# GpSimd's two gathers of a step, moved from the step's head to behind its first and second subtraction

## What is computed

```python
e = jnp.stack([tbl_0[ids[:, 0]], ..., tbl_31[ids[:, 31]]], axis=1)      # 1024 x 32 x 64
for i in range(2):                                                       # x0 = h = e
    z = jnp.einsum('bhd,bmd->bhmd', h, x0).reshape(batch, H * M, dim)
    out = jax.nn.relu(jnp.einsum('bcd,oc->bod', z, Ws[i]) + bs[i][None, :, None])
    # first layer: out[:, :64] is the next h, out[:, 64:] is a result; second: all of out
z = jnp.sum(jnp.concatenate(finals, axis=1), axis=-1)
h = jnp.concatenate([z, dense_ctx], axis=1)
h = relu(h @ W_top1 + b_top1); h = relu(h @ W_top2 + b_top2); y = h @ W_top3
```

## Time and profile before

| | |
|---|---|
| median of three runs | 1965.58 us (1965.43 to 1966.08) |
| the profiled execution | 1965.55 us, span 1963.7 us |
| PE busy | 1929.8 us (98%) |
| DVE busy | 1914.1 us (97%) |
| POOL busy | 1826.8 us (93%) |
| ACT busy | 1729.9 us (88%) |
| POOL L299, subtractions | 384, 1581.7 us |
| POOL L265, gathers from `idx` | 240, 228.3 us |

### The profile page before, as it was taken

How to read it: one execution, slowest core, us unless ns; L and a number is a source line. 1 busy time by engine, 2 the same in 40 slices (tenths; PEclk the granted TensorE clock), 3 DMA queues, 4 the chain that set the end, 5 groups by cost and what they waited for, 6 DMA issues and landing times.

```text
span 1963.7 us, 28730 instructions
## 1 busy us (share of the span) xinstructions
PE 1929.8 (98%) x7240; PEld 1361.8 (69%) x7240; DVE 1914.1 (97%) x1246; ACT 1729.9 (88%) x1959; POOL 1826.8 (93%) x646
## 2 busy tenths in 40 slices
PE   3999999999999999999999999999999999999999
PEld 2667777777776776776776777677677677677776
DVE  5999999999999999999999999999999999999995
ACT  4889998998998998998899899899899899889986
POOL 4999999999999999999999999999999999999883
PEclk8999999999999999999999999999999999999999
DMA  8987777777777777787787787787778777777730
GB/s 215 239 212 188 198 187 186 196 191 184 194 194 181 196 193 180 194 194 186 192 196 187 185 197 192 181 196 194 181 193 197 183 191 194 188 187 196 187 93 1
DMA packets 277281, 364.27 MB, mean 185 GB/s; under 512 B 116353, under 2 KB 116737, under 8 KB 277138
## 3 DMA queue, kind: packets, MB, share of 16 engines
q1 hardware_dynamic: 265730, 352.74, 72.7%
q0 software_dynamic: 8192, 8.40, 1.9%
q10 hardware_dynamic: 3344, 2.96, 0.6%
HBM read 347.02 MB, written 16.78 MB: 185 GB/s over the span
## 4 chain that ended last, share of the span: by engine, by line
PE 96%; DMA 1%; ACT 1%; POOL 1%; DVE 1%; issue 1%; ACTq 0%; DVEq 0%
PE out L814 22%; PE out L839 21%; PE out L833 21%; PE out L832 21%; PE out L822 7%; PE out L816 2%; POOL zl L299 1%; PE hrep L880 0%; DMA xrep<-fields_dram 0%; DMA left_x<-fields_dram 0%; ACT hrep L486 0%; ACT zh L473 0%; PE xr L880 0%; PE lz L880 0%; DVE zl L774 0%
## 5 line engine op out<-in xcount | busy, mean ns | idle before, releaser
L299 POOL TENSOR_TENSOR zl<-prod,zh 128x2048 fp32r<-128x2048 f32 (+2 forms) x384 | 1581.7, 4150 | 45.2 <-ACT zh L473 43.3
L832 PE MATMUL out<-zh,w1h 128*128 128x512 f32 x1888 | 736.6, 390 | 0.8 <-ACT relu L479 0.8
L833 PE MATMUL out<-zh,w1l 128*128 128x512 f32 x1888 | 736.7, 390 | 0.0
L473 ACT ACTIVATE zh<-prod 128x2048 fp32r<-128x2048 f32 (+2 forms) x384 | 664.9, 1732 | 17.3 <-DVE prod L719 9.4
L486 ACT ACTIVATE hrep<-out,b_sb 32x512 f32<-32x512 f32 (+1 forms) x768 | 496.2, 646 | 139.2 <-PE out L816 129.4
L839 PE MATMUL out<-zl,w1h 128*128 128x512 f32 x1888 | 565.9, 418 | 0.6 <-POOL zl L299 0.6
L814 PE MATMUL out<-prod,w_sb 128*128 128x512 f32 x1024 | 464.8, 597 | 27.2 <-DVE prod L650 22.3
L839 PEld LDWEIGHTS out<-zl,w1h 128*128 128x128 f32 x1888 | 354.4, 188 | 128.6 <-issue 61.5
L832 PEld LDWEIGHTS out<-zh,w1h 128*128 128x128 f32 x1888 | 354.7, 188 | 103.3 <-issue 30.4
L833 PEld LDWEIGHTS out<-zh,w1l 128*128 128x128 f32 x1888 | 354.4, 188 | 76.4
L814 PEld LDWEIGHTS out<-prod,w_sb 128*128 128x128 f32 x1024 | 195.2, 191 | 224.4 <-issue 214.6
(11 more groups left out here) (69 smaller groups left out, 721.3 us busy)
## 6 DMA issues: line engine op xcount, KB each, us to landing
rot_low<-fields_dram SPq DMA_DIRECT2D x512, 256.0 KB, 6.2
rot_high<-fields_dram SPq DMA_DIRECT2D x512, 256.0 KB, 4.2
xrep<-fields_dram SPq DMA_DIRECT2D x252, 128.0 KB
left_y<-fields_dram SPq DMA_DIRECT2D x256, 64.0 KB, 2.2
fields_dram<-emb SPq DMA_DIRECT2D x504, 32.0 KB, 4.5
left_x<-fields_dram SPq DMA_DIRECT2D x252, 64.0 KB, 2.3
emb<-in_tables,idx POOLq DMA_INDIRECT x244, 3.6
w_sb<-in_w SPq DMA_DIRECT2D x1, 1024.0 KB, 5.8
```

Source lines behind the costliest of these rows:

```text
L299: pool.tensor_tensor(zl[u][:, 0:size, :], product[:, 0:size, :], zh[u][:, 0:size, :].bitcast(F32), ALU.subtract).then_inc(zl_made[u], 1)
L473: act.activation(zh[u][:, 0:size, :], product[:, 0:size, :], ACT.Copy).then_inc(zh_made[u], 1)
L832: nc.tensor.matmul(out1[:, :], w1h[:, k, :], zh[u][:, t, :], start=start and t == 0, stop=False)
L833: nc.tensor.matmul(out1[:, :], w1l[:, k, :], zh[u][:, t, :], start=False, stop=False)
```

## The change

In `step` of GpSimd, `gathers` is called twice with one gather each instead of once with two. Of the step's two gathers the first now stands behind the subtraction of part 0 and the second behind that of part 1. The waits of an even step (`scratch_written`, `idx_loaded`) and the increment of `gather_started` go with its first gather. Step 0 had its first subtraction ahead of the gathers already. Nothing changes on another engine, and no instruction is added or removed.

```diff
-            def gathers(i, c):
+            def gathers(i, c, k):
                 n, b = i * 2 + c // 2 + AHEAD, (c // 2 + AHEAD) % 2
                 if known(i) and n == AHEAD:
-                    if c % 2 == 0:
+                    if c % 2 == 0 and k == 0:
                         pool.wait_ge(scratch_written[b], AHEAD // 2 * WRITTEN)
                     rows = known_rows(n)
                 else:
-                    if c % 2 == 0:
+                    if c % 2 == 0 and k == 0:
                         pool.wait_ge(scratch_written[b], written(b, i + (c // 2 + AHEAD) // 2))
...
-                for g in range(c % 2 * 2, c % 2 * 2 + 2):
-                    gather(b, rows, g)
+                gather(b, rows, c % 2 * 2 + k)
...
-                first = known(m) and m == 0
-                if first:
-                    low_part(0, 0, in_parts(0, 0), prod[1])
-                if is_up_to(i, c, LAST - 2 * AHEAD):
-                    gathers(i, c)
-                if not first:
-                    low_part(m, 0, in_parts(0, c), prod[1])
+                gathering = is_up_to(i, c, LAST - 2 * AHEAD)
+                low_part(m, 0, in_parts(0, c), prod[1])
+                if gathering:
+                    gathers(i, c, 0)
                 low_part(m, 1, in_parts(1, c), prod[2])
+                if gathering:
+                    gathers(i, c, 1)
                 low_part(m, 2, in_parts(2, c), prod[3])
```

## The result

The changed kernel took 1984.88 us (median of six runs, 1984.05 to 1985.55), the kernel before 1965.67 us (1965.28 to 1966.08). The ratio of the two is 1.0098 with a 95% interval of 1.0088 to 1.0108: 19.2 us slower. The forecast was 1981.7 us.

The account below looks back on a forecast made before the run. TensorE, without a gap in a 59.31 us turn, was taken to set the pace, with GpSimd nearly as full. 30 turns x 0.54 = 16.2 us added to 1965.55 gave 1981.7 us, range 1965.3 to 1992.

Parts of the forecast that it names:

- What bounds: Loop turn of 59.31 us: TensorE has no gap and sets the pace; GpSimd, busy 56.95 us, is nearly as full.
- GpSimd's pitch and the third part's place: GpSimd's step: first-subtraction pitch falls from 15.00 to 14.94 us; third part ends 14.99 us after first start, not 12.61.
- L(3): Start of the L814 matmuls on TensorE that make the first-layer output of step c = 3; the hand count's zero.
- The stall's price: When TensorE waits for GpSimd's third part zl2: 0.85 us from its end to the L814 matmuls, from one start-up row.
- Per turn: TensorE waits for GpSimd's zl at c = 3 (0.38 us) and c = 0 (0.16 us): 0.54 us more each turn.
- The sum: Whole run: 30 turns x 0.54 = 16.2 us on top of 1965.55 us gives 1981.7 us (+0.8%).
- a few us once in the start-up: Most that the later write and loads in SP's queue were said to cost; taken as zero.
- SP: SP's queue: the write of the gathered block comes some 4.5 us late, with loads behind it; cost taken as zero.
- The other readers stay covered: VectorE's products that overwrite zl1's input or wait for zl2 were said to start after GpSimd's results are done.
- the ring: Loop through ScalarE, two steps of GpSimd and TensorE, said to set the turn, 0.54 us longer than before.
- No change: Rival: GpSimd's third part still comes in time if c = 0's ends 0.54 us sooner; 1965.6 us, chance 0.17.
- A longer step: Rival: 0.30 us follows every gather on GpSimd, turn up to 1.66 us longer; 1990 to 2015 us, chance within 0.10.

Follow-up runs that it names:

- the control with the first swap: The kernel before, with ScalarE's rounding of part 0 (zh0) put ahead of its copy of xr in each step: 1979.37 us.
- the first swap on ScalarE: The changed kernel, with ScalarE's rounding of part 0 (zh0) put ahead of its copy of xr in each step: 1981.62 us.
- the run with c = 1 and c = 2 alone: The changed kernel, but only steps c = 1, c = 2 and step 0 keep the new gather order; c = 3 and c = 0 have both gathers first: 1967.39 us.

## Why the prediction was right, step by step

- **What bounds.** TensorE without a gap and GpSimd next to full: right. But the busy time of 59.31 of 59.31 us, from which the prediction read "no gap", couldn't have shown one: the control with the first swap has TensorE busy for 59.80 of 59.80 us in a turn that is 0.5 us longer. What shows it is the 1.7 us that TensorE's weight loads waited for GpSimd in the whole run. Three engines next to full had more to it than I used: VectorE at 59.16 of 59.31 us is what the first swap on ScalarE ran into.
- **GpSimd's pitch and the third part's place.** Said: the third part ends 14.99 behind the first one's start, a gather has 0.16 ahead and 0.02 behind. Measured 14.99, 0.16, and 0.00 to 0.03. The first subtraction of c = 3 at L(3) + 14.10; measured 14.11. GpSimd's wait ahead of it, said 1.0, measured 1.02.
- **The stall's price.** 0.85 us from the third part's end to the L814 group, from one place in the start-up. Measured in the turn: 1059.19 - 1058.34 = 0.85, where the end of the third part, 1058.34, is worked out from its length in another row. From the start of the weight load, which is a row, it is 0.80 in both places (1059.19 - 1058.39, and 54.72 - 53.92 in the earlier trace rows). The Trainium skill (TensorE: Matmul & The Clock Gate, Part 2) says that TensorE pulls weight loads ahead of running matmuls; had that held at this place, the price would be an estimated 0.74. The trace doesn't agree here: the weight loads of the L837 groups began 0.05 us behind the result that they multiply, and 0.85 holds.
- **Per turn.** Said 0.38 at c = 3 and 0.16 at c = 0, in sum 0.54. Measured 0.39 and 0.17, 0.56.
- **The sum, short by 3 us.** Two terms. The average turn is longer than the one looked at: an L812 group starts at 130.79 and another 28.75 turns later at 1852.87 (the same two are at 129.00 and 1833.73 before), 59.90 us a turn, so 0.60 in place of 0.54, some 1.7 us over 29 turns. And the first turn cost 1.79 (130.79 against 129.00), not 0.54, 1.25 more. There the same thing happened to a step c = 2: GpSimd waited 1.83 us for zh0 and had both gathers still before it. ScalarE's wait for an xrep load is longer there than before (2.02 us against 1.62), but it isn't needed for the loss: in the run with c = 1 and c = 2 alone it is 1.63, and the same group starts at 130.81. The prediction had named "a few us once in the start-up", for SP's sake, and taken zero.
- **SP.** Said: the write is 4.5 us late, cost zero. Measured 7.6 us late, cost zero: right about the cost, too low for the lateness. The 3.6 us from issue to landing was a median over all gathers; from the start of a block's last gather (at c = 1, 1023.95 in this trace) to the write it was 7.2. SP's margin ahead of xrep was used up, as its waits show, and the 13 us behind it were not.
- **The other readers stay covered.** Right for VectorE's products. One more wait came up that I hadn't listed: VectorE's L672 waits for zh3, 13.2 us in 33 times against four times for 5.0 us before; it stands beside the ring. The kernel with the copy moved to ScalarE's idle place still has 34 such waits, 12.1 us in all, and its turns average 59.37 us against 59.30 before, so they cost at most 0.07 us a turn there.
- **The rivals.** No change: the margin of 0.54 us that it needed wasn't there. A longer step: the gap behind a gather was 0.02, so it fell too.

## What to carry to other kernels

Work that stands ahead of a wait may be cover, and costs nothing there. Before moving it, find out what the engine would do in its place; if it would wait, then the move adds the whole length to whatever comes behind, here 2.38 us to the third result. With several engines next to full, follow one turn through the engines by hand, from the row of the input that comes last to the row of the reader that is ready first, and compare the length of the ring with the turn; the shares of busy time show neither. Work out the first turn apart: here it lost 1.8 us, three times what the others did.

## What I had not expected

TensorE's busy time hides its stalls. In the changed kernel's turn, the row of busy times (stretch, length, PE, PEld, DVE, ACT, POOL, granted clock, DMA share, GB/s) is

```profile
1044.02:1103.88 59.86, 59.75 (x224) 41.78 (x223) 59.35 (x39) 53.16 (x61) 57.42 (x21) 1.00 0.77 190
```

Of 0.56 us that TensorE loses there, the matmul column shows 0.11. The ends of matmuls are modelled in this profile, and the modelled time covers the rest; the weight-load rows show the waits, 0.54 and 0.29 us ahead of them. The granted clock was 1.00 in this turn, the 2.4 GHz level, and its mean over the run was 0.997 with the 60 stalls as without them.

A copy of 0.60 us on an engine that is busy for 88% of the run cost 13.7 us when it was moved behind the one rounding that followed it, and nothing when it was moved a few instructions further, to a place where the engine waits.
